# A windowed nearest-neighbour attention block: keys as weights, and half of a masked add moved from VectorE to ScalarE and GpSimd

## Chip, cores, metric

One core of a Trainium2 chip runs the whole kernel. The metric is device time of one launch in microseconds. Engines are called PE (TensorE), DVE (VectorE), ACT (ScalarE), POOL (GpSimd) and SP (SyncE).

## What is computed

The block works on x of shape 8 x 1024 x 128. Layer norm and modulation come first, then the attention that matters here, for each of 8 heads of width 16; a routed mixture of linear experts follows. The part around the change, cut to its core:

```python
q_h = relu(h @ enc_q[h]); v_h = relu(h @ enc_v[h])
k_windows = q_h[:, idx, :]              # the 64 tokens up to and with t
diff = k_windows - q_h[:, :, None, :]
dist = sqrt((diff * diff * m_h).sum(-1) + 1e-8)
neg_d, loc = top_k(-dist, 32)           # the 32 nearest of 64
infl = exp(-topd); infl = infl / (infl.sum(-1) + 1e-8)
context = einsum('btk,btkd->btd', infl, neighbor_v)
context = context + gate * 0.1 * heb_ctx
out = q_h * context                     # then @ decoder, residual, norm, experts
```

## The kernel before

After a prologue (norm, projections, routing) the tokens are worked in 64 chunks of 128. All engines run a software pipeline written out by hand: step i of an engine's `step` function holds work of chunks i-3 to i+3, in a fixed order, and semaphores are all that ties the engines. A buffer has two copies (index s) or four (s4). An engine takes its instructions strictly in order, so an instruction that waits holds up all behind it.

The way of one chunk k, with the lines of the profile:

- PE writes squared distances of 128 queries to 192 keys, for 8 heads, into psD (`distances`, L1142 and L1145). A mask is added by a first matmul. For each query, the 64 keys of its window lie in an outer block (64 columns; left for the first 64 queries, right for the rest) and in the middle block. Of each column pair exactly one belongs to the window. The mask adds 1e30 to the one that doesn't, and -1e30 to the token itself.
- ACT copies the outer blocks through Relu into `key` (L666, L667), and the q part into `qh` (L686).
- DVE takes the minimum of `key` and the middle block, all eight heads in one instruction of 512 columns out of PSUM (L1012). This stands in the middle of step k-1, after two of the four rounds of picking.
- ACT forms `key` = (distance squared) to the power 1/4 with a Ln and an Exp (L701, L727).
- DVE, step k: four rounds of MAX8 (L979, 8 heads) and MATCH_REPLACE (L990, 8 heads) take out the 32 largest keys, which are the 32 farthest, and put -1e4 in their place in `work`. Semaphore `picked` tells when four heads are through.
- ACT, step k+1: Square and Exp(-x) of `work`, four heads at a time (L628, L635, `square` and `weights`), give exp(-distance) for the near ones and 0 for those taken out.
- POOL, step k+1: `unfold` (L452) spreads four heads' weights over 128 key columns.
- PE transposes these weights (L1161), ACT copies them out (L642, `to_wts`), PE multiplies them with the values (L1175).
- ACT copies the context (`cst`, L714, L715) and forms 1/sum with a Ln and an Exp (`den` L717, `rden` L733).
- POOL, step k+1: context times q (`t1`, L481), and the Hebbian part in two products (`t2`, L483, L485); step k+2: `t1` times `rden` (L461), plus `t2` (L465), to `osp`, which goes to the decoder on PE.

In step i POOL's order is L461, L465 (chunk i-2), two unfolds (i-1), `sqs` L475 (i+3), L481, L483, L485 (i-1), `selm` L491 (i+3), `hsc` L497 (i), `sst` L502 (i+3), and two small ones, L509 and L510 (i+2). ACT's order in step i begins with square and weights of chunk i-1, then `h2T` (L658), the outer copies of chunk i+1, `yo` (L673), and so on. ACT's waits for the right to overwrite `key` and for `yo` read:

```python
act.wait_ge(dist_ready, k + 1)
need(act, picked, 16 * (k - 2) + 4)
```

The second is reached when the first of the four rounds has read `key` of chunk k-2.

## Time and profile before

| What | us |
|---|---|
| Median of 3 runs | 816.1 |
| Lowest and highest run | 813.3, 819.37 |
| The profiled execution, its time | 814.3 |
| Its span, first to last instruction | 812.5 |
| DVE busy | 759.0 |
| PE busy | 705.3 |
| ACT busy | 678.9 |
| POOL busy | 465.8 |
| DVE in the chain that ended last | 83% of the span |

Start times are from the span's start. A record of DVE, ACT or PE can run a little past the start of the next one, since instructions are pipelined; what an instruction costs a busy engine is the distance from its start to the next start. The row of an instruction that waited says in brackets how long and for whom. The granted TensorE clock was 0.958 of full speed over the span and 1.00 in the steady part.

### The profile page before, as it was taken

The numbers are of one execution on the slowest core, as the hardware profiler recorded it, in microseconds if no ns is written. First come the engines' busy times: TensorE is split into PE (matmuls) and PEld (weight loads), VectorE is DVE, ScalarE is ACT, GpSimd is POOL, SyncE is SP. The second block draws the span as 40 slices with busy tenths as digits, with TensorE's granted clock in tenths as the row PEclk, the third lists the DMA queues.
The fourth block names the chain that finished last, engine by engine and source line by source line (L and its number), as shares of the span: only waits on it lengthen the run. The fifth ranks groups of instructions, "written<-read, shape, count | busy, mean of one in ns | idle before, by whom it ended". The sixth has DMA issues, their size and how long they took to land.

```text
span 812.5 us, 21167 instructions
## 1 busy us (share of the span) xinstructions
PE 705.3 (87%) x4437; PEld 577.8 (71%) x4437; DVE 759.0 (93%) x6490; ACT 678.9 (84%) x2182; POOL 465.8 (57%) x871
## 2 busy tenths in 40 slices
PE   5987989999898889988988899889888998898844
PEld 3445667777777777777777777777777777777743
DVE  5956899999999999999999999999999999999980
ACT  3981359988888998898989988898999888988964
POOL 2112456666666666666666666666666666666541
PEclk9995989999999999999999999999999999999955
DMA  5310000111111001111110011111100111111000
GB/s 171 107 31 10 25 17 27 32 32 32 33 31 31 27 26 32 32 32 32 31 31 27 26 32 33 33 31 31 31 25 29 32 31 32 32 31 31 19 4 10
DMA packets 49232, 27.23 MB, mean 34 GB/s; under 512 B 5513, under 2 KB 48593, under 8 KB 49105
## 3 DMA queue, kind: packets, MB, share of 16 engines
q1 hardware_dynamic: 49104, 25.90, 10.9%
q14 instruction: 92, 0.75, 0.3%
q8 instruction: 36, 0.59, 0.3%
HBM read 10.28 MB, written 4.19 MB: 18 GB/s over the span
## 4 chain that ended last, share of the span: by engine, by line
DVE 83%; PE 9%; ACT 2%; DMA 2%; issue 1%; POOL 1%; SPq 1%; ACTq 0%; POOLq 0%
DVE work L990 46%; DVE m L979 30%; DVE key L1012 5%; DMA big<-in_x 1%; PE psD L1145 1%; DVE key L801 1%; PE psD L1050 1%; DVE st_p L792 1%; PE psC L1175 1%; PE psC L1078 1%; PE psW L1232 1%; PE psW L1161 1%; DMA wmod_sb<-in_wmod 1%; POOL big L452 1%; PE psX L1133 0%
## 5 line engine op out<-in xcount | busy, mean ns | idle before, releaser
L990 DVE MATCH_REPLACE8 work<-m,work 128x64 f32<-128x64 f32 x1536 | 301.0, 208 | 0.0
L1145 PE MATMUL psD<-sst,tst 128*128 128x224 f32 x1024 | 238.7, 356 | 0.0
L979 DVE MAX8 m<-work 128x8 f32<-128x64 f32 x1536 | 211.5, 210 | 0.0
L1145 PEld LDWEIGHTS psD<-sst,tst 128*128 128x128 f32 x1024 | 196.5, 192 | 3.1 <-issue 0.3
L452 POOL TENSOR_TENSOR big<-work,con 128x512 f32<-128x512 f32 x128 | 162.2, 1290 | 20.5 <-ACT work L635 15.9
L481 POOL TENSOR_TENSOR t<-cst,qh 128x128 f32<-128x128 f32 x64 | 27.7, 433 | 213.2 <-ACT cst L715 213.2
L1175 PE MATMUL psC<-vst,big 128*128 128x34 f32 x1024 | 127.5, 270 | 0.0
L1175 PEld LDWEIGHTS psC<-vst,big 128*128 128x128 f32 x1024 | 126.8, 195 | 0.2
L990 DVE MATCH_VALUE_LOAD work<-m,work 128x8 f32 x1536 | 122.3, 80 | 0.0
L990 DVE MATCH_REPLACE8 work<-m,key 128x64 f32<-128x64 f32 x512 | 100.2, 208 | 0.0
L1142 PE MATMUL psD<-mask_bf,ident_bf 128*128 128x448 bf16 x256 | 91.5, 357 | 1.8 <-DMA tst<-nst 1.8
L1161 PE MATMUL psW<-con,big 128*128 128x128 f32 x512 | 79.9, 280 | 2.9 <-POOL big L452 2.9
L701 ACT ACTIVATE key<-key,bias 128x512 f32<-128x512 f32 x64 | 46.2, 722 | 40.2 <-DVE key L1012 40.2
L642 ACT ACTIVATE big<-psW 128x512 f32<-128x512 f32 x128 | 76.1, 595 | 3.1 <-PE psW L1161 2.9
L1232 PE MATMUL psW<-sqs,selm 128*8 128x192 f32 x256 | 53.3, 332 | 21.9 <-POOL selm L491 21.9
L979 DVE MAX8 m<-key 128x8 f32<-128x64 f32 x512 | 70.5, 209 | 0.0
L1161 PEld LDWEIGHTS psW<-con,big 128*128 128x128 f32 x512 | 58.6, 144 | 4.2 <-POOL big L452 4.1
L502 POOL TENSOR_TENSOR sst<-qT_all,aS 128x384 f32<-128x384 f32 x64 | 53.1, 830 | 12.4 <-PE psD L1145 12.4
L635 ACT ACTIVATE work<-work 128x256 f32<-128x256 f32 x128 | 53.4, 417 | 4.1
L1232 PEld LDWEIGHTS psW<-sqs,selm 128*8 128x8 f32 x256 | 17.9, 89 | 54.2 <-POOL selm L491 41.1
L1183 PE MATMUL psX<-x,con 128*128 128x128 f32 x128 | 32.5, 337 | 27.0 <-ACT h2T L658 27.0
L475 POOL TENSOR_TENSOR sqs<-qT_all 128x384 f32<-128x384 f32 x64 | 54.1, 846 | 1.6 <-ACT qT_all L565 1.5
(200 smaller groups left out, 1473.6 us busy)
## 6 DMA issues: line engine op xcount, KB each, us to landing
hst<-hT_all SPq DMA_DIRECT2D x64, 96.0 KB
tst<-qT_all SPq DMA_DIRECT2D x256, 17.0 KB
big<-in_x SPq DMA_DIRECT2D x16, 256.0 KB, 2.8
tst<-nst SPq DMA_DIRECT2D x256, 1.0 KB
xs<-in_x SPq DMA_DIRECT2D x64, 64.0 KB, 1.9
out<-yo SPq DMA_DIRECT2D x64, 64.0 KB, 1.7
sst<-nst SPq DMA_DIRECT2D x128, 3.0 KB
con<-in_consts SPq DMA_DIRECT2D x1, 549.5 KB, 6.7
```

The source lines that it names most:

```text
L452: nc.gpsimd.tensor_tensor(wun[:, s, heads].rearrange("p h (v j) -> p h v j", v=2), work[:, s].rearrange("p (h j) -> p h j", h=NH)[:, heads ...
L475: nc.gpsimd.tensor_tensor(sqs[:, s], win, win, ALU.mult).then_inc(opnd_ready, 1)
L502: nc.gpsimd.tensor_tensor(sst[:, s, :, 0:3 * WIN], qT_all[:, :, bass.ds(column(k), 3 * WIN)], aS[:, :, bass.ds(k // CPB, 1)].broadcast_to( ...
L635: nc.scalar.activation(wk, wk, ACT.Exp, scale=-1.0).then_inc(wsel_ready, 1)
L642: nc.scalar.activation(wts[:, (i - 1) % 2, 4 * w:4 * w + 4].rearrange("p h t -> p (h t)"), psW[:, w], ACT.Copy).then_inc(wts_ready, 1)
L979: last = v.max(m8[:, h], src[:, h * WIN:(h + 1) * WIN])
L990: last = v.match_replace(work[:, s, cols], m8[:, h], src[:, cols], GONE)
L1142: mm(bank_of(r)[:, :, 0:SW], ident_bf[:], mask_bf[:].unsqueeze(1).broadcast_to([P, NG, SW]), start=True, stop=False, skip_group_check=True)
L1145: last = mm(bank_of(r)[:, g, 0:SW], tst[:, s, r, g], sst[:, s, g], start=False, stop=(g == NG - 1), skip_group_check=True)
L1161: nc.tensor.transpose(psW[:, w, (h % 4) * P:(h % 4 + 1) * P], wun[:, s, h], ident).then_inc(wt_ready, 1)
L1175: last = mm(pC[:, h * 2 * VD:(h + 1) * 2 * VD], wts[:, s, h], vst[:, s4, h].rearrange("p v e -> p (v e)"), start=True, stop=True)
L1232: mm(pN, selm[:, s, g], sqs[:, s, g], start=(g == 0), stop=(g == NG - 1))
```

## The change

The functions named below are those of POOL, ACT, DVE and PE in this order; GONE and C_MASK stand at the top.

The key becomes exp(-distance), formed by Ln, Exp(0.5 x) and Exp(-x), so that the 32 largest keys are the nearest. What is taken out is replaced by 0, and the weights are `key` minus `work`, a subtraction on POOL ahead of each unfold; the Square and Exp behind the picking go. The mask is -1e30 throughout: Relu turns the column outside the window into 0, and the minimum becomes a sum. For heads 0 to 3 ACT copies the middle block through Relu into `work`, and POOL adds it to `key`; for heads 4 to 7 DVE adds it from PSUM. The product with q is taken once, after the sum of context and Hebbian part, and not twice.

```diff
-GONE = -1e4
+GONE = 0.0
+ON_POOL = 4
...
-    c[:, C_MASK:C_MASK + 3 * WIN] = np.concatenate([first, middle, last], 1)
+    c[:, C_MASK:C_MASK + 3 * WIN] = -np.abs(np.concatenate([first, middle, last], 1))
...
                         need(pool, wt_ready, 8 * (k - 2) + 4 * w + 4)
+                        heads = slice(4 * w, 4 * w + 4)
+                        wk = work[:, s, w * 4 * WIN:(w + 1) * 4 * WIN]
+                        pool.wait_ge(picked, 16 * k + 15 + w)
+                        nc.gpsimd.tensor_tensor(wk, key[:, s, w * 4 * WIN:(w + 1) * 4 * WIN], wk, ALU.subtract).then_inc(wsel_ready, 1)
                         pool.wait_ge(wsel_ready, 2 * k + 1 + w)
...
-                k, s = i - 2, (i - 2) % 2
+                k, s, s4 = i - 2, (i - 2) % 2, (i - 2) % 4
                 if there(i, -2):
+                    q = qh[:, s4, :, 0:HD]
                     pool.wait_ge(rden_ready, k + 1)
-                    pool.wait_ge(t1_done, k + 1)
-                    nc.gpsimd.tensor_tensor(t1[:].rearrange(h3, h=NH), t1[:].rearrange(h3, h=NH), rden[:, s].unsqueeze(2).broadcast_to([P, NH, HD]), ALU.mult).then_inc(ctx_done, 1)
+                    pool.wait_ge(t2_done, k + 1)
+                    nc.gpsimd.tensor_tensor(t1[:].rearrange(h3, h=NH), cst[:, s, :, 0:HD], rden[:, s].unsqueeze(2).broadcast_to([P, NH, HD]), ALU.mult).then_inc(t1_done, 1)
+                    pool.wait_ge(t1_done, 2 * k + 1)
+                    nc.gpsimd.tensor_tensor(t1[:], t1[:], t2[:, s], ALU.add).then_inc(t1_done, 1)
                     need(pool, po_ready, k - 1)
-                    pool.wait_ge(t2_done, 2 * (k + 1))
-                    pool.wait_ge(ctx_done, k + 1)
-                    nc.gpsimd.tensor_tensor(osp[:, s], t1[:], t2[:], ALU.add).then_inc(osp_ready, 1)
+                    pool.wait_ge(t1_done, 2 * k + 2)
+                    nc.gpsimd.tensor_tensor(osp[:, s].rearrange(h3, h=NH), t1[:].rearrange(h3, h=NH), q, ALU.mult).then_inc(osp_ready, 1)
                 unfold(0)
                 unfold(1)
+
+                k, s = i + 1, (i + 1) % 2
+                if there(i, 1):
+                    pool.wait_ge(outer_ready, 2 * (k + 1))
+                    pool.wait_ge(mid_ready, k + 1)
+                    nc.gpsimd.tensor_tensor(key[:, s, 0:ON_POOL * WIN], key[:, s, 0:ON_POOL * WIN], work[:, s, 0:ON_POOL * WIN], ALU.add).then_inc(d2_ready, 1)
...
-                    q, hb = qh[:, s4, :, 0:HD], qh[:, s4, :, HD:2 * HD]
-                    pool.wait_ge(cst_ready, 2 * (k + 1))
-                    nc.gpsimd.tensor_tensor(t1[:].rearrange(h3, h=NH), cst[:, s, :, 0:HD], q, ALU.mult).then_inc(t1_done, 1)
+                    hb = qh[:, s4, :, HD:2 * HD]
+                    pool.wait_ge(qhs_ready, k + 1)
                     pool.wait_ge(hsc_done, k + 1)
-                    nc.gpsimd.tensor_tensor(t2[:].rearrange(h3, h=NH), hb, hsc[:, s].unsqueeze(2).broadcast_to([P, NH, HD]), ALU.mult).then_inc(t2_done, 1)
-                    pool.wait_ge(t2_done, 2 * k + 1)
-                    nc.gpsimd.tensor_tensor(t2[:].rearrange(h3, h=NH), t2[:].rearrange(h3, h=NH), q, ALU.mult).then_inc(t2_done, 1)
+                    nc.gpsimd.tensor_tensor(t2[:, s].rearrange(h3, h=NH), hb, hsc[:, s].unsqueeze(2).broadcast_to([P, NH, HD]), ALU.mult).then_inc(t2_done, 1)
...
-                square(0)
-                weights(0)
-                square(1)
-                weights(1)
...
-                    need(act, picked, 16 * (k - 2) + 4)
+                    need(act, wsel_ready, 2 * (k - 1))
                     e = key[:, s].rearrange("p (h j) -> p h j", h=NH)
                     nc.scalar.activation(e[0:WIN], pH[0:WIN, :, 0:WIN], ACT.Relu).then_inc(outer_ready, 1)
                     nc.scalar.activation(e[WIN:P], pH[WIN:P, :, 2 * WIN:3 * WIN], ACT.Relu).then_inc(outer_ready, 1)
+                    need(act, w_ready, 2 * (k - 1))
+                    nc.scalar.activation(work[:, s, 0:ON_POOL * WIN].rearrange("p (h j) -> p h j", j=WIN), pH[:, 0:ON_POOL, WIN:2 * WIN],
+                                         ACT.Relu).then_inc(mid_ready, 1)
...
                     act.wait_ge(d2_ready, k + 1)
+                    act.wait_ge(d2b_ready, k + 1)
                     nc.scalar.activation(key[:, s], key[:, s], ACT.Ln, bias=bias[:, 1:2]).then_inc(ln_done, 1)
...
+                    act.wait_ge(ln_done, k + 1)
+                    nc.scalar.activation(key[:, s], key[:, s], ACT.Exp, scale=0.5).then_inc(dist_done, 1)
...
+                    act.wait_ge(dist_done, k + 1)
+                    nc.scalar.activation(key[:, s], key[:, s], ACT.Exp, scale=-1.0).then_inc(key_ready, 1)
...
-                    nc.scalar.activation(key[:, s], key[:, s], ACT.Exp, scale=0.25).then_inc(key_ready, 1)
...
-                    need(act, ctx_done, k - 1)
+                    need(act, osp_ready, k - 1)
                     nc.scalar.activation(rden[:, s], den[:, s], ACT.Exp, scale=-1.0).then_inc(rden_ready, 1)
...
+                    dve.wait_ge(mid_ready, k + 1)
                     dve.wait_ge(qhs_ready, k + 1)
-                    e = key[:, s].rearrange("p (h j) -> p h j", h=NH)
-                    v.scalar_tensor_tensor(out=e, in0=pH[:, :, WIN:2 * WIN], scalar=0.0, in1=e, op0=ALU.max, op1=ALU.min).then_inc(d2_ready, 1)
+                    e = key[:, s].rearrange("p (h j) -> p h j", h=NH)[:, ON_POOL:NH]
+                    v.scalar_tensor_tensor(out=e, in0=pH[:, ON_POOL:NH, WIN:2 * WIN], scalar=0.0, in1=e, op0=ALU.max, op1=ALU.add).then_inc(d2b_ready, 1)
...
-                    need(pe, d2_ready, k)
+                    need(pe, mid_ready, k)
+                    need(pe, qhs_ready, k)
+                    need(pe, d2b_ready, k)
```

On POOL, the beginning of a steady step before the change (`t` stands for t1 or t2, `big` for the unfolded weights `wun`), each with the semaphores it waits for:

```order
L461 TENSOR_TENSOR t<-t,rden 128x128 [waits t1_done,rden_ready]
L465 TENSOR_TENSOR osp<-t 128x128 [waits ctx_done,t2_done,po_ready]
L452 TENSOR_TENSOR big<-work,con 128x512 [waits wsel_ready,wt_ready] x2
L475 TENSOR_TENSOR sqs<-qT_all 128x384 [waits pn_ready]
L481 TENSOR_TENSOR t<-cst,qh 128x128 [waits cst_ready]
L483 TENSOR_TENSOR t<-qh,hsc 128x128 [waits hsc_done]
L485 TENSOR_TENSOR t<-t,qh 128x128 [waits t2_done]
```

The same place after the change:

```order
L467 TENSOR_TENSOR t<-cst,rden 128x128 [waits t2_done,rden_ready]
L469 TENSOR_TENSOR t<-t 128x128 [waits t1_done]
L472 TENSOR_TENSOR osp<-t,qh 128x128 [waits t1_done,po_ready]
L455 TENSOR_TENSOR work<-key,work 128x256 [waits picked,wt_ready]
L457 TENSOR_TENSOR big<-work,con 128x512 [waits wsel_ready]
L455 TENSOR_TENSOR work<-key,work 128x256 [waits picked,wt_ready]
L457 TENSOR_TENSOR big<-work,con 128x512 [waits wsel_ready]
L482 TENSOR_TENSOR key<-key,work 128x256 [waits mid_ready,outer_ready]
L488 TENSOR_TENSOR sqs<-qT_all 128x384 [waits pn_ready]
L495 TENSOR_TENSOR t<-qh,hsc 128x128 [waits hsc_done,qhs_ready]
```

A product moved from the middle to the front, a subtraction stands ahead of each unfold, an addition that waits for ACT stands behind them, and nothing waits for `cst` any more.

On ACT, the copies of the distances in a steady step before, from the picking's results to `qh`:

```order
L628 ACTIVATE work<-work 128x256 [waits picked]
L635 ACTIVATE work<-work 128x256 [waits square_done]
L628 ACTIVATE work<-work 128x256 [waits picked]
L635 ACTIVATE work<-work 128x256 [waits square_done]
L658 ACTIVATE h2T<-psX,modT 128x128 [waits y_ready,pn2_ready]
L666 ACTIVATE key<-psD 64x512 [waits picked,dist_ready]
L667 ACTIVATE key<-psD 64x512
L673 ACTIVATE yo<-psX 128x128 [waits out_in0,y_ready]
```

And after:

```order
L646 ACTIVATE h2T<-psX,modT 128x128 [waits y_ready,pn2_ready]
L654 ACTIVATE key<-psD 64x512 [waits wsel_ready,dist_ready]
L655 ACTIVATE key<-psD 64x512
L657 ACTIVATE work<-psD 128x256 [waits w_ready]
L664 ACTIVATE yo<-psX 128x128 [waits out_in0,y_ready]
L638 ACTIVATE big<-psW 128x512 [waits c_ready,wt_ready]
L671 ACTIVATE oT<-psX 128x128 [waits po_ready]
L677 ACTIVATE qh<-psD 128x256 [waits osp_ready,dist_ready]
```

Four instructions went, one came, and the outer copies and the new middle copy wait for POOL's subtractions and unfolds.

Further on in the same step of ACT, from the key's Ln to `rden`, after the change:

```order
L693 ACTIVATE key<-key,bias 128x512 [waits d2b_ready,d2_ready]
L698 ACTIVATE x,sum_c<-psX,bias 128x128 [waits att_ready]
L704 ACTIVATE key<-key 128x512 [waits ln_done]
L711 ACTIVATE cst<-psC 64x136 [waits osp_ready,c_ready]
L712 ACTIVATE cst<-psC 64x136
L714 ACTIVATE den<-cst,bias 128x8 [waits cst_ready]
L719 ACTIVATE key<-key 128x512 [waits dist_done]
L724 ACTIVATE nm_c<-sum_c 128x1 [waits x2_ready]
L730 ACTIVATE rden<-den 128x8 [waits osp_ready,den_done]
```

Before, the same stretch held one Exp of `key` instead of two, between `nm_c` and `rden`.

## Rows read from the trace of the kernel before

**Rows 1.** The page: busy time, share of the span and instructions of each engine.

```profile
PE 705.3 (87%) x4437; PEld 577.8 (71%) x4437; DVE 759.0 (93%) x6490; ACT 678.9 (84%) x2182; POOL 465.8 (57%) x871
```

**Rows 2.** Busy time of each engine in stretches, the first the ramp, the others ten steps.

```profile
core 0: us, PE busy (x) PEld busy (x) DVE busy (x) ACT busy (x) POOL busy (x), PEclk, DMA share, GB/s
109.00:205.00 96.00, 87.45 (x566) 73.88 (x567) 94.55 (x848) 83.49 (x270) 61.58 (x116) 0.97 0.09 28
205.00:313.50 108.50, 97.68 (x661) 83.10 (x660) 108.50 (x971) 98.09 (x320) 70.24 (x131) 1.00 0.10 30
...
639.00:747.50 108.50, 97.65 (x662) 83.15 (x662) 108.50 (x971) 98.06 (x321) 70.24 (x131) 1.00 0.10 31
```

**Rows 3.** Waits of POOL: engine, line, waited for: us in total, times, longest.

```profile
POOL t L481 <- ACT cst L715: 213.2, 64, 6.6
```

**Rows 4.** Timeline of DVE, one step: start us, us, engine line op out<-in.

```profile
408.84 1.11 DVE L979 MAX8 m<-key 128x8 f32<-128x64 f32 x8
...
413.97 0.69 DVE L1012 SCALAR_TENSOR_TENSOR key<-psD,key 128x512 f32<-128x512 f32 x1
414.57 1.11 DVE L979 MAX8 m<-work 128x8 f32<-128x64 f32 x8
...
418.79 0.22 DVE L990 MATCH_REPLACE8 work<-m,work 128x64 f32<-128x64 f32 x1
...
419.70 1.11 DVE L979 MAX8 m<-key 128x8 f32<-128x64 f32 x8
```

**Rows 5.** Timeline of POOL in the same step; in brackets the idle time before.

```profile
409.75 2.54 POOL L452 TENSOR_TENSOR big<-work,con 128x512 f32<-128x512 f32 x2
412.24 0.83 POOL L475 TENSOR_TENSOR sqs<-qT_all 128x384 f32<-128x384 f32 x1
416.31 0.43 POOL L481 TENSOR_TENSOR t<-cst,qh 128x128 f32<-128x128 f32 x1 [3.24 <-ACT cst L715]
416.70 0.40 POOL L483 TENSOR_TENSOR t<-qh,hsc 128x128 f32<-128x128 f32 x1
417.18 0.45 POOL L485 TENSOR_TENSOR t<-t,qh 128x128 f32<-128x128 f32 x1
...
419.49 0.40 POOL L461 TENSOR_TENSOR t<-t,rden 128x128 f32<-128x128 f32 x1
420.06 0.46 POOL L465 TENSOR_TENSOR osp<-t 128x128 f32<-128x128 f32 x1 [0.17 <-POOL t L461]
420.60 2.52 POOL L452 TENSOR_TENSOR big<-work,con 128x512 f32<-128x512 f32 x2
```

**Rows 6.** Timeline of ACT in the same step.

```profile
410.61 0.58 ACT L666 ACTIVATE key<-psD 64x512 f32<-64x512 f32 x1
...
411.83 0.28 ACT L673 ACTIVATE yo<-psX 128x128 f32<-128x128 f32 x1
...
412.76 0.38 ACT L686 ACTIVATE qh<-psD 128x256 f32<-128x256 f32 x1
413.04 0.60 ACT L642 ACTIVATE big<-psW 128x512 f32<-128x512 f32 x1
...
413.83 0.21 ACT L696 ACTIVATE rnn<-lnn 128x8 f32<-128x8 f32 x1
414.69 0.72 ACT L701 ACTIVATE key<-key,bias 128x512 f32<-128x512 f32 x1 [0.66 <-DVE key L1012]
...
415.95 0.28 ACT L715 ACTIVATE cst<-psC 64x136 f32<-64x136 f32 x1
...
416.57 0.61 ACT L727 ACTIVATE key<-key 128x512 f32<-128x512 f32 x1
417.09 0.19 ACT L733 ACTIVATE rden<-den 128x8 f32<-128x8 f32 x1
```

**Rows 7.** Timeline of PE in the same step.

```profile
414.99 0.35 PE L1142 MATMUL psD<-mask_bf,ident_bf 128*128 128x448 bf16 x1
...
420.31 0.92 PE L1145 MATMUL psD<-sst,tst 128*128 128x224 f32 x4
```

More of the change, by code:

```diff
@@ L172, in adaln_block @@
         t1 = sb("t1", [P, NH * HD])
-        t2 = sb("t2", [P, NH * HD])
+        t2 = sb("t2", [P, 2, NH * HD])
         osp = sb("osp", [P, 2, NH * HD])
@@ L269, in adaln_block @@
         outer_ready = sem("outer_ready")
+        mid_ready = sem("mid_ready")
         d2_ready = sem("d2_ready")
+        d2b_ready = sem("d2b_ready")
         ln_done = sem("ln_done")
@@ L275, in adaln_block @@
         picked = sem("picked")
-        square_done = sem("square_done")
+        dist_done = sem("dist_done")
         wsel_ready = sem("wsel_ready")
@@ L294, in adaln_block @@
         t2_done = sem("t2_done")
-        ctx_done = sem("ctx_done")
         osp_ready = sem("osp_ready")
@@ L449, in unfold @@
                         need(pool, wt_ready, 8 * (k - 2) + 4 * w + 4)
+                        heads = slice(4 * w, 4 * w + 4)
+                        wk = work[:, s, w * 4 * WIN:(w + 1) * 4 * WIN]
+                        pool.wait_ge(picked, 16 * k + 15 + w)
+                        nc.gpsimd.tensor_tensor(wk, key[:, s, w * 4 * WIN:(w + 1) * 4 * WIN], wk, ALU.subtract).then_inc(wsel_ready, 1)
                         pool.wait_ge(wsel_ready, 2 * k + 1 + w)
-                        heads = slice(4 * w, 4 * w + 4)
                         nc.gpsimd.tensor_tensor(
@@ L622, in step @@
             def step(i):
-                def square(w):
-                    if there(i, -1):
-                        wk = work[:, (i - 1) % 2, w * 4 * WIN:(w + 1) * 4 * WIN]
-                        act.wait_ge(picked, 16 * (i - 1) + 15 + w)
-                        nc.scalar.activation(wk, wk, ACT.Square).then_inc(square_done, 1)
-                def weights(w):
-                    if there(i, -1):
-                        wk = work[:, (i - 1) % 2, w * 4 * WIN:(w + 1) * 4 * WIN]
-                        act.wait_ge(square_done, 2 * (i - 1) + 1 + w)
-                        nc.scalar.activation(wk, wk, ACT.Exp, scale=-1.0).then_inc(wsel_ready, 1)
                 def to_wts(w):
@@ L707, in step @@
                                          accum_out=sum_c[:, s:s + 1]).then_inc(x2_ready, 1)
+                k, s = i + 1, (i + 1) % 2
+                if there(i, 1):
+                    act.wait_ge(ln_done, k + 1)
+                    nc.scalar.activation(key[:, s], key[:, s], ACT.Exp, scale=0.5).then_inc(dist_done, 1)
                 k, s = i - 1, (i - 1) % 2
@@ L717, in step @@
                     nc.scalar.activation(den[:, s], cst[:, s, :, HD], ACT.Ln, bias=bias[:, 1:2]).then_inc(den_done, 1)
+                k, s = i + 1, (i + 1) % 2
+                if there(i, 1):
+                    act.wait_ge(dist_done, k + 1)
+                    nc.scalar.activation(key[:, s], key[:, s], ACT.Exp, scale=-1.0).then_inc(key_ready, 1)
                 k, s = i - 2, (i - 2) % 2
@@ L722, in step @@
                     nc.scalar.activation(nm_c[:], sum_c[:, s:s + 1], ACT.Copy, scale=-1.0 / D).then_inc(nm_done, 1)
-                k, s = i + 1, (i + 1) % 2
-                if there(i, 1):
-                    act.wait_ge(ln_done, k + 1)
-                    nc.scalar.activation(key[:, s], key[:, s], ACT.Exp, scale=0.25).then_inc(key_ready, 1)
                 k, s = i - 1, (i - 1) % 2
```

## Prediction

> **What bounds the kernel now.** I read the page's busy times first. DVE leads with 93% of the span, ahead of PE with 87% [rows 1]; a share over the span can't say who holds up whom. The busy times by stretch can: from 205 us to 747 us DVE is busy for 108.50 of 108.50 us, ten steps at a time, with PE at 97.7, ACT at 98.1, POOL at 70.2 and the granted clock at 1.00 [rows 2]. In the ramp, 109 to 205 us, DVE had 1.45 us idle [rows 2]. One step lasts 419.70 - 408.84 = 10.86 us on DVE's timeline [rows 4]; ten steps give 10.85, and I use that. So DVE alone sets the pace. Everything else has slack, POOL most: it waits 213 us in total for `cst`, 3.24 us of each step [rows 3, 5].
>
> **DVE by itself.** The instruction that shrinks from 512 to 256 columns starts at 413.97, and the next starts at 414.57, so it costs 0.60 us [rows 4]. Its duration less the fixed part goes by columns. I take 0.34 us for half (bounds: 0.30, the plain half, and 0.60, unchanged). The 64 searches and replacements of a step are untouched; what is replaced, and by what, changes no shape. DVE's own step becomes 10.85 - 0.26 = 10.59 us. If nothing else moved, the kernel would gain 64 x 0.26 = 17 us.
>
> **What now closes in a ring.** Before, ACT could copy the outer blocks of chunk i+1 as soon as the distances were there. Its wait for `picked` was for the first round of chunk i-1, long past. After, `key` and `work` of chunk i-1 are read by POOL after the picking, so in step i the outer copies wait for both subtractions, and the middle copy waits for both unfolds. Behind this middle copy in ACT's queue stand `yo`, both weight copies, `qh`, the Ln, both Exps, `cst`, `den` and `rden`. POOL's first instruction of step i+1 waits for `rden` of step i, and the next subtraction stands three instructions behind it. So POOL's step i releases ACT's step i, which releases POOL's step i+1: a ring with no DVE in it. Its length is a lower bound for the step, so I add it up. S is the start of the first subtraction.
>
> POOL, from S to the end of the second unfold. The subtraction on 128x256 is not in this trace. Its bounds are 0.40 us, the product on 128x128, and 0.83, the one on 128x384 [rows 5]. Half of an unfold of 512 columns (2.54/2 = 1.27 each) is 0.64, about midway, and I take it. A POOL instruction that waits for the one before it starts late: the product at 416.70 lasts 0.40, and its follower starts at 417.18, 0.08 late [rows 5]. The unfolds start 2.49/2 = 1.25 us apart [rows 5]. Sum: 0.64 + 0.08 + 1.25 + 0.64 + 0.08 + 1.27 = 3.96.
>
> The Trainium skill bears on this term ("GPSIMD Engine Reference", section 3.1): a two-input tensor_tensor on GPSIMD takes about 2.6 cycles of 1.2 GHz per element, and section 4.1 advises VectorE for elementwise adds, about twice as fast. Estimated from that page, 256 columns take 0.55 us before any fixed part; with 0.55 in both places the ring below would be 0.18 shorter, and the kernel 11 us faster than my sum. The rows agree with its direction: POOL pays 0.64 for the add for which DVE saves 0.26.
>
> Hand-over to ACT: I take 0.08, that of ACT to POOL, whose `cst` record ends at 415.95 + 0.28 = 416.23 while POOL starts at 416.31 [rows 5, 6]. The outer copies don't count: they start after the second subtraction, last 411.83 - 410.61 = 1.22 [rows 6], and the unfold beside them takes 1.35 with its hand-over. The ring goes through the unfold.
>
> ACT, from the middle copy to the end of `rden`. The middle copy is 128x256 out of PSUM, like `qh`, whose follower starts 413.04 - 412.76 = 0.28 later [rows 6]; the other end is half of the two outer copies, 0.61. I take 0.28 for the equal shape. From `yo` at 411.83 to the end of `rnn` at 413.83 + 0.21 it is 2.21 [rows 6]; today ACT then idles 0.66 for DVE [rows 6], which here falls into the ring. From the Ln at 414.69 to `rden` at 417.09 it is 2.40; `rden` lasts 0.19; the second Exp costs what the first does, 417.09 - 416.57 = 0.52 [rows 6]. Sum: 0.28 + 2.21 + 2.40 + 0.52 + 0.19 = 5.60. Then 0.08 back to POOL.
>
> POOL, from `rden` to the next subtraction: 0.40 + 0.08 for the first product, 0.46 for the add, with a gap of 0.17 as ahead of today's `osp`, and 420.60 - 420.06 = 0.54 for the third [rows 5]. Sum 1.65.
>
> Ring: 3.96 + 0.08 + 5.60 + 0.08 + 1.65 = 11.37 us, against 10.85 today and 10.59 for DVE alone.
>
> **Does anything on the ring wait still longer?** DVE's half: `qh` ends 412.76 + 0.38 - 411.83 = 1.31 after `yo` starts, so at S + 3.96 + 0.08 + 0.28 + 1.31 = S + 5.63, and DVE can add at S + 5.68. With 0.34 it is done at S + 6.02, before ACT comes to the Ln at S + 6.53. POOL's add, ready 0.64 + 0.08 after the middle copy, is earlier. From the add to the next step DVE needs 419.70 - 414.57 = 5.13 [rows 4], so the next step starts at S + 11.15. The first half of the picks is out 419.70 - 418.79 - 0.22 = 0.69 before the end, at S + 10.46, and POOL wants it at S + 11.37. DVE is off the ring by 0.9 us, and has 11.37 - 10.59 = 0.78 us idle per step, at its add, waiting for `qh`. PE: from the first distances at 414.99 to the end of the last at 420.31 + 0.92 it is 6.24 [rows 7]. The first distances keep their place 414.99 - 411.83 = 3.16 behind `yo`, since all ahead of them hangs on `yo` and the weight copies as before. So the distances end 9.40 behind `yo`, and the outer copies want them 11.37 - 0.28 - 1.35 = 9.74 behind it. That is 0.34 of slack, and the wait of PE for `selm` inside the stretch goes, since `selm` no longer stands behind `cst`. POOL itself: 1.65 and 3.96 on the ring, then 0.08 + 0.38 + 0.08 for the middle copy, 0.64 for the add, 0.83 for `sqs`, 0.48 for `t2`, and 419.49 - 417.18 - 0.41 = 1.90 for `selm` to `n2g` [rows 5] make 10.0, which is 1.4 short of the ring; its wait for `cst` (3.24) is gone. ACT has its remaining 2.8 us (norm, `vst`, `nst`, `h2T`) beside POOL's part and idles there.
>
> **Sum.** The ring holds from step 2, the first with a `rden` to wait for, to step 62, the last with a next chunk: 61 steps x (11.37 - 10.85) = +31.7 us. Steps 0 and 1 run at DVE's new pace: -0.5. DVE's lead over POOL, 0.9, is used up once: -0.9. The 1.45 us that DVE idled in the ramp [rows 2] falls together with the new waits: -1.5. The prologue and the tail I put at nothing: one more Exp and a POOL add ahead of chunk 0 (+1.2) against Squares and Exps that go in the tail (about -1). Total +28.8. The profiled execution took 814.3, so it would take 843.1. The median of the runs lay 1.8 above it: 845 us.
>
> **Ends of the unknown costs.** Subtractions at 0.40 or 0.83: -0.48 or +0.38 per step. Middle copy at 0.61: +0.33. The four gaps and hand-overs of 0.08 at nothing or at 0.17: -0.32 or +0.36. All low gives 10.57, all high 12.44. They won't err together: I hold 11.1 to 11.7 likely, which is 829 to 865 us.
>
> **Rivals.** (A) DVE stays the bound. For it speaks that DVE is the only full engine today, and that its load shrinks by 0.26; against it, that the ring would have to be 0.78 shorter than its rows. Below a ring of 10.59 the time is 816.1 - 16.6 = 799.5, faster than before. It takes almost all low ends together: chance 0.07. (B) The ring comes out near today's step, 10.7 to 11.0, because gaps that I counted overlap: then losses and savings cancel within 1%, which is about what a measurement of this kernel can tell from no change. About 817 us, chance 0.09. (C) The ring is longer, by subtractions at 0.83 and a middle copy at 0.61: 11.37 + 0.38 + 0.33 = 12.08, 61 x 1.23 - 2.9 = +72, 888 us. Against it is the shape of `qh`. With cases in between, chance 0.07. (D) PE idles longer in one piece per step (after the first transposes, until `yo`, over 1 us against 0.34 now), and the granted clock falls from 1.00. Then PE, 97.7 of 108.5 us busy at full clock [rows 2], would itself set a step beyond 12 us: over 890 us, chance 0.02.
>
> **How the numbers follow.** The forecast has 0.75. Slower by over 1% is the forecast, C and D: 0.84; within 1% is B: 0.09; faster is A: 0.07. The range goes from 818, about the middle of B, to 866, the top of the likely ring; 0.07 + 0.04 lies below and 0.09 above.
>
> **What would show it.** Right: DVE busy about 93% in the steady stretches, its idle time at the new add (L1010), put down to ACT's `qh` copy; ACT idle ahead of the outer or middle copy, waiting for POOL; POOL idle ahead of L467, waiting for `rden`, instead of `cst`; a step of 11.2 to 11.6 us. Wrong: DVE still without idle time between 205 and 740 us; POOL waiting for `picked`; a POOL subtraction far from 0.64; or a second wait inside the ring, ahead of the Ln or of `cst`.

## The result, and the profile after

The changed kernel takes 879.38 us (median of 4 runs, 877.85 to 882.29) against 814.95 us for the kernel before (813.3 to 819.37). The ratio is 1.081, with a 95% interval of 1.077 to 1.084: slower, as forecast, but by 64 us where 29 were forecast, and outside the range of 818 to 866 us. The profiled execution spans 878.3 us; its granted TensorE clock is 0.892 where it was 0.958. All ratios below are to the kernel before, run beside each variant; its medians lay between 812.2 and 815.8 us.

The page of the changed kernel: busy times, the chain, and the groups with idle time ahead of them (busy, mean ns of one | idle before, and for whom).

```profile
PE 743.5 (85%) x4437; PEld 630.4 (72%) x4437; DVE 744.7 (85%) x6490; ACT 651.5 (74%) x2054; POOL 575.3 (66%) x999
...
PE 34%; POOL 27%; ACT 26%; issue 8%; DVE 3%; DMA 2%; ACTq 0%; POOLq 0%; SPq 0%; DVEq 0%
...
L467 POOL TENSOR_TENSOR t<-cst,rden 128x128 f32<-128x128 f32 x64 | 25.7, 401 | 116.0 <-ACT rden L730 116.0
L482 POOL TENSOR_TENSOR key<-key,work 128x256 f32<-128x256 f32 x64 | 46.9, 733 | 81.4 <-ACT work L657 81.4
...
L1190 PE MATMUL psX<-con,osp 128*128 128x128 f32 x64 | 19.6, 307 | 94.7 <-ACT yo L664 94.7
L455 POOL TENSOR_TENSOR work<-key,work 128x256 f32<-128x256 f32 x128 | 93.3, 729 | 2.3 <-PE psX L1131 2.3
L1010 DVE SCALAR_TENSOR_TENSOR key<-psD,key 128x256 f32<-128x256 f32 x64 | 27.2, 425 | 78.4 <-ACT qh L677 78.4
```

DVE, 93% busy in [rows 1], is down to 85%, and the chain that ended last runs over PE, POOL and ACT instead. The waits stand where the ring has its joints: POOL waits for `rden` (116.0 us, in place of the 213 us for `cst` of [rows 3]), and its add for the middle copy; DVE waits 78.4 us at its add for `qh`. One wait I had passed over quickly is large too: PE idles 94.7 us ahead of the transpose of `osp` (L1190, called the osp transpose below), until ACT has copied `yo`. And L455, the subtraction, lasts 729 ns.

Busy times of the changed kernel by stretch, columns as in [rows 2]: one of 108.5 us, then two steps that follow each other, from `yo` to `yo`.

```profile
core 0: us, PE busy (x) PEld busy (x) DVE busy (x) ACT busy (x) POOL busy (x), PEclk, DMA share, GB/s
205.00:313.50 108.50, 94.51 (x597) 83.24 (x596) 95.97 (x872) 84.78 (x272) 78.91 (x136) 0.91 0.09 27
```

```profile
403.53:414.74 11.21, 9.43 (x66) 8.40 (x66) 9.80 (x89) 9.31 (x31) 8.73 (x15) 1.00 0.10 30
414.74:428.56 13.82, 12.73 (x66) 11.40 (x66) 11.57 (x106) 9.65 (x32) 8.76 (x15) 0.75 0.08 23
```

and a piece of the second of them:

```profile
416.90:422.50 5.60, 5.60 (x23) 5.36 (x24) 5.60 (x53) 3.72 (x14) 2.46 (x8) 0.50 0.10 30
```

In [rows 2] the steady stretches had a granted clock of 1.00. Here it is 0.91. The two single steps show why: the first lasts 11.21 us at 1.00, the next 13.82 at 0.75, with a piece of 5.60 us at 0.50. I call a step at 1.00 throughout a full-clock step, and the stretch at 0.50 a fall of the clock. So the steps are of several kinds. From the starts of `yo` (L664) in ACT's timeline I took the length of all steps up to the last few: 59 steps, of which 39 last 11.20 to 11.24 us, one 11.40, 15 last 13.8, and 4 last 12.2. Nearly all steps of the kernel before last 10.84 to 10.87 us. The account: 59 x (11.22 - 10.85) = 21.8 us for the longer step, and 15 x 2.58 + 4 x 0.95 = 42.5 us for steps with a fall of the clock, together 64.3 us. The medians differ by 64.4 us, the spans of the two profiled executions by 65.8; ramp and tail make up the small rest.

The full-clock step, and the slow one behind it, on ACT:

```profile
403.53 0.27 ACT L664 ACTIVATE yo<-psX 128x128 f32<-128x128 f32 x1
...
405.64 0.71 ACT L693 ACTIVATE key<-key,bias 128x512 f32<-128x512 f32 x1
...
408.54 0.19 ACT L730 ACTIVATE rden<-den 128x8 f32<-128x8 f32 x1
...
413.18 0.59 ACT L654 ACTIVATE key<-psD 64x512 f32<-64x512 f32 x1 [1.13 <-POOL work L455]
...
414.46 0.38 ACT L657 ACTIVATE work<-psD 128x256 f32<-128x256 f32 x1
414.74 0.27 ACT L664 ACTIVATE yo<-psX 128x128 f32<-128x128 f32 x1
...
427.05 0.59 ACT L654 ACTIVATE key<-psD 64x512 f32<-64x512 f32 x1 [0.48 <-PE psD L1143]
...
428.56 0.27 ACT L664 ACTIVATE yo<-psX 128x128 f32<-128x128 f32 x1
```

and the same ring on POOL:

```profile
408.81 0.40 POOL L467 TENSOR_TENSOR t<-cst,rden 128x128 f32<-128x128 f32 x1 [1.38 <-ACT rden L730]
...
410.30 0.73 POOL L455 TENSOR_TENSOR work<-key,work 128x256 f32<-128x256 f32 x1
411.11 1.28 POOL L457 TENSOR_TENSOR big<-work,con 128x512 f32<-128x512 f32 x1
412.35 0.73 POOL L455 TENSOR_TENSOR work<-key,work 128x256 f32<-128x256 f32 x1
413.16 1.27 POOL L457 TENSOR_TENSOR big<-work,con 128x512 f32<-128x512 f32 x1
```

These rows give the ring term by term. From the first subtraction (410.30) to the middle copy (414.46) it is 4.16 us, where I had 3.96 + 0.08. From there to `yo` 0.28, as taken. From `yo` (403.53) to the Ln (405.64) 2.11 for 2.21, and from the Ln to the end of `rden` (408.73) 3.09 for 3.11. Then 0.08 to POOL, and from L467 (408.81) to the subtraction (410.30) 1.49 for 1.65. Sum 11.21 for 11.37.

In the slow step the joint is another one. ACT's outer copy at 427.05 waits 0.48 us for PE, not for POOL as at 413.18. PE shows what happened:

```profile
411.58 0.92 PE L1143 MATMUL psD<-sst,tst 128*128 128x224 f32 x4
...
415.16 0.30 PE L1190 MATMUL psX<-con,osp 128*128 128x128 f32 x1 [1.78 <-ACT yo L664]
...
419.82 1.70 PE L1143 MATMUL psD<-sst,tst 128*128 128x224 f32 x4
```

The four distance matmuls of one bank took 0.92 us at 411.58; at 419.82, after the idle time of 1.78 us, they took 1.70. In the full-clock step PE's last distances end 411.58 + 0.92 - 403.53 = 8.97 behind `yo`, and ACT's outer copies start 413.18 - 403.53 = 9.65 behind it, so 0.68 us is to spare. In the slow step ACT can start only 427.05 - 414.74 = 12.31 behind `yo`, because PE isn't done. With 1.51 for the outer and middle copies that makes 13.82.

The idle time before the osp transpose is not the same in all steps. In PE's timeline it is 1.8 us, as the 1.78 above, in nearly all of the 40 steps that follow a full-clock one, and 1.1 us in the 19 that follow a slow one; the mean of 1.55 (94.7 / 61) mixes the two. Of the 40, 19 are slow; of the 19, none.

### The profile page after: what moved, and what is told of

Same layout as the page of the kernel before. It is cut to its first block, busy times and chain, and to the rows that moved or that the text cites. A ratio compares the mean times of both kernels' runs of the same rounds, so it can differ in the third digit from the quotient of the medians.

```text
span 878.3 us, 21484 instructions
## 1 busy us (share of the span) xinstructions
PE 743.5 (85%) x4437; PEld 630.4 (72%) x4437; DVE 744.7 (85%) x6490; ACT 651.5 (74%) x2054; POOL 575.3 (66%) x999
## 4 chain that ended last, share of the span: by engine, by line
PE 34%; POOL 27%; ACT 26%; issue 8%; DVE 3%; DMA 2%; ACTq 0%; POOLq 0%; SPq 0%; DVEq 0%
POOL big L457 13%; PE psD L1143 10%; POOL work L455 7%; PE psC L1173 6%; ACT big L638 5%; ACT key L693 3%; ACT key L719 3%; PE psD L1140 3%; ACT key L704 2%; PE psW L1232 2%; POOL t L469 2%; POOL osp L472 2%; PE psW L1219 2%; POOL t L467 2%; ACT qh L677 2%
## 5 line engine op out<-in xcount | busy, mean ns | idle before, releaser
L1143 PE MATMUL psD<-sst,tst 128*128 128x224 f32 x1024 | 262.2, 383 | 0.0
L1143 PEld LDWEIGHTS psD<-sst,tst 128*128 128x128 f32 x1024 | 214.6, 210 | 7.2 <-issue 0.3
L1173 PE MATMUL psC<-vst,big 128*128 128x34 f32 x1024 | 144.5, 291 | 2.7 <-ACT big L638 2.7
L1173 PEld LDWEIGHTS psC<-vst,big 128*128 128x128 f32 x1024 | 144.4, 218 | 3.1 <-issue 3.1
L467 POOL TENSOR_TENSOR t<-cst,rden 128x128 f32<-128x128 f32 x64 | 25.7, 401 | 116.0 <-ACT rden L730 116.0
L482 POOL TENSOR_TENSOR key<-key,work 128x256 f32<-128x256 f32 x64 | 46.9, 733 | 81.4 <-ACT work L657 81.4
L1190 PE MATMUL psX<-con,osp 128*128 128x128 f32 x64 | 19.6, 307 | 94.7 <-ACT yo L664 94.7
L455 POOL TENSOR_TENSOR work<-key,work 128x256 f32<-128x256 f32 x128 | 93.3, 729 | 2.3 <-PE psX L1131 2.3
L1010 DVE SCALAR_TENSOR_TENSOR key<-psD,key 128x256 f32<-128x256 f32 x64 | 27.2, 425 | 78.4 <-ACT qh L677 78.4
L1190 PEld LDWEIGHTS psX<-con,osp 128*128 128x128 f32 x64 | 9.1, 143 | 107.5 <-issue 107.5
L654 ACT ACTIVATE key<-psD 64x512 f32<-64x512 f32 x64 | 37.8, 591 | 62.0 <-POOL work L455 46.6
```

What stands on the lines that cost most here:

```text
L455: nc.gpsimd.tensor_tensor(wk, key[:, s, w * 4 * WIN:(w + 1) * 4 * WIN], wk, ALU.subtract).then_inc(wsel_ready, 1)
L467: nc.gpsimd.tensor_tensor(t1[:].rearrange(h3, h=NH), cst[:, s, :, 0:HD], rden[:, s].unsqueeze(2).broadcast_to([P, NH, HD]), ALU.mult).then ...
L482: nc.gpsimd.tensor_tensor(key[:, s, 0:ON_POOL * WIN], key[:, s, 0:ON_POOL * WIN], work[:, s, 0:ON_POOL * WIN], ALU.add).then_inc(d2_ready, 1)
L1143: last = mm(bank_of(r)[:, g, 0:SW], tst[:, s, r, g], sst[:, s, g], start=False, stop=(g == NG - 1), skip_group_check=True)
L1173: last = mm(pC[:, h * 2 * VD:(h + 1) * 2 * VD], wts[:, s, h], vst[:, s4, h].rearrange("p v e -> p (v e)"), start=True, stop=True)
```

## Experiments

**The gap filled (e1).** The first question was whether PE's idle time brings the clock down. Against the changed kernel, on PE behind `weights_T(0)`:

```diff
+                if there(i, -3) and there(i, -1):
+                    need(pe, cst_ready, 2 * (i - 1))
+                    for _ in range(12):
+                        nc.tensor.transpose(psC[:, 0:P], ident, ident)
```

> The changed kernel, and PE runs 12 idle transposes of the identity into psC (their output is never read) after the first weight transposes, where it waits for ACT's copy yo. Theory (ring of POOL and ACT of 11.22 us per step, and on top of it a fall of the granted clock brought on by PE's idle stretch ahead of the osp transpose): the 15 steps of 13.80 us and the 5 of 12.17 us become 11.22 us, so 15 x 2.58 + 5 x 0.95 = 43 us less than 879, about 836 us, clock near 0.96. Rival 1 (the clock falls for another reason, such as the lower load of PE over the step): 870 us or more. Rival 2 (the transposes cost what they last, 1.3 us per step, since PE is on the path): 879 + 80 = 960 us.

Measured: 838.03 us, ratio 1.032 (1.027 to 1.037). All steady steps lie between 11.21 and 11.40 us. Ten steps' worth of time, and what is left of the wait:

```profile
422.00:530.50 108.50, 103.39 (x758) 93.74 (x757) 102.62 (x933) 90.10 (x288) 84.24 (x145) 1.00 0.10 30
```

```profile
PE psX L1195 <- ACT yo L664: 30.6, 61, 0.7
```

The clock is at 1.00 and 41 us of the 64 are gone, although PE does 1.3 us more per step. Rival 2 falls. Rival 1 is not excluded by this run alone, since the transposes fill the gap and raise PE's load over the step at once (103.39 of 108.50 us busy, for 94.51); e2 and the last two runs bear on it. The ring's part, the step of 11.24, is untouched.

**The ring opened (e2).** The second question was whether the two waits for overwriting are what closes the ring. The buffer for the middle block lies in a tile of the prologue (`wmod_sb`), since SBUF was full, and so does now `sq_c`, a small work buffer of the norm. Chunk k has its key in `key[:, k % 3]`; against the changed kernel:

```diff
-        key = sb("key", [P, 2, NH * WIN])
+        key = sb("key", [P, 3, NH * WIN])
...
+        midb = wmod_sb[:, 0:2 * ON_POOL * WIN].rearrange("p (s c) -> p s c", s=2)
...
-                    need(act, wsel_ready, 2 * (k - 1))
+                    need(act, wsel_ready, 2 * (k - 2))
...
-                    need(act, w_ready, 2 * (k - 1))
+                    need(act, d2_ready, k - 1)
-                    nc.scalar.activation(work[:, s, 0:ON_POOL * WIN].rearrange("p (h j) -> p h j", j=WIN), pH[:, 0:ON_POOL, WIN:2 * WIN],
+                    nc.scalar.activation(midb[:, s].rearrange("p (h j) -> p h j", j=WIN), pH[:, 0:ON_POOL, WIN:2 * WIN],
```

> The changed kernel with three copies of key and a buffer of its own for the middle block, so that ACT's copies in step i wait for nothing that POOL does in step i. Instructions and their order are those of the changed kernel. Theory (the two overwrite waits close the ring): DVE is full again at 10.59 us per step, PE's idle stretch goes and the granted clock stays at 1.00; 64 x 0.26 = 17 us below before, 798 to 804 us. Rival (the later weights, by way of subtraction, unfold, transposes, contexts and rden, or POOL's load of 10 us a step, set the pace by themselves): a step of 11 us or more, 825 us or more.

Measured: 807.38 us, ratio 0.993 (0.990 to 0.996). The same instructions in the same order, 72 us faster than with two copies of `key`. But it is 3 us over the expected range, and the clock was not at 1.00 throughout:

```profile
422.00:530.50 108.50, 96.94 (x662) 85.78 (x663) 108.05 (x991) 95.74 (x303) 88.28 (x152) 0.98 0.11 31
```

```profile
346.93 0.27 ACT L665 ACTIVATE yo<-psX 128x128 f32<-128x128 f32 x1
...
359.14 0.27 ACT L665 ACTIVATE yo<-psX 128x128 f32<-128x128 f32 x1
```

DVE is nearly full. Most steps last 10.5 to 10.6 us; five of 58 last 12.2, as that from 346.93 to 359.14. PE still idled 1.07 us a step ahead of the osp transpose (65.5 us in 61 waits).

This run also says something on rival 1 above. A full-clock step of the kernel before, with its three waits on PE, and then one of e2:

```profile
411.83:422.68 10.85, 9.77 (x67) 8.32 (x66) 10.85 (x99) 9.81 (x33) 7.04 (x14) 1.00 0.10 30
```

```profile
417.86 0.82 PE L1232 MATMUL psW<-sqs,selm 128*8 128x192 f32 x4 [0.36 <-POOL selm L491]
...
421.61 0.49 PE L1183 MATMUL psX<-x,con 128*128 128x128 f32 x2 [0.38 <-ACT h2T L658]
...
423.10 0.30 PE L1192 MATMUL psX<-con,osp 128*128 128x128 f32 x1 [0.34 <-ACT yo L673]
```

```profile
390.68:401.19 10.51, 9.43 (x66) 8.40 (x66) 10.51 (x98) 9.37 (x31) 8.63 (x16) 1.00 0.10 30
```

PE is busy for 90% of the step in both, and idle for 1.08 us in both. Before, this idle time stands in three places and no step is slow; in e2 it stands in one, and five are. So a lower load of PE over the step isn't needed for a fall; what differs is how the idle time is spread. Of the growth from 0.34 to 1.07 us the middle copy ahead of `yo` accounts for about 0.27 (0.61 in e3, below); the rest is what PE no longer waits elsewhere.

**Both at once (e5).** So I filled that gap too, with 8 transposes.

> e2_no_ring and 8 idle transposes of PE ahead of the osp transpose, where it idles 1.07 us a step. Theory: the 7 steps of 12.2 us in e2 were falls of the clock behind that idle stretch and go; all steps 10.5 to 10.6 us, 807 - 7 x 1.6 = 796 us, clock 0.96 or more. Rival (those steps come from something else, or 0.9 us more of PE's work delays the path): 807 us or more.

Measured: 796.67 us, ratio 0.980 (0.976 to 0.983): faster than both kernels. DVE is full and the clock at 1.00:

```profile
422.00:530.50 108.50, 106.38 (x759) 95.28 (x758) 108.50 (x996) 96.47 (x306) 89.75 (x154) 1.00 0.11 31
```

The five long steps are gone; all steady ones last 10.51 to 10.69. PE is at 106.38 of 108.50, so there is little room for more such filling. That the time came out at the expected 796 is in part luck: the expectation counts seven long steps in e2, where the trace has five, 8.6 us longer together. The profiled spans differ by 10.0 us, of which 6.4 lie in the 58 steady steps and 3.5 ahead of them.

**One part alone (e3).** The half add was then put into the kernel before, with a buffer of its own for the middle block. POOL adds behind `unfold(1)`, ACT copies behind the outer copies, and DVE adds heads 4 to 7; against the kernel before:

```diff
-    c[:, C_MASK:C_MASK + 3 * WIN] = np.concatenate([first, middle, last], 1)
+    c[:, C_MASK:C_MASK + 3 * WIN] = -np.abs(np.concatenate([first, middle, last], 1))
...
+                    pool.wait_ge(mid_ready, k + 1)
+                    nc.gpsimd.tensor_tensor(key[:, s, 0:ON_POOL * WIN], key[:, s, 0:ON_POOL * WIN], midb[:, s], ALU.add).then_inc(d2p_ready, 1)
...
+                    need(act, d2p_ready, k - 1)
+                    nc.scalar.activation(midb[:, s].rearrange("p (h j) -> p h j", j=WIN), pH[:, 0:ON_POOL, WIN:2 * WIN],
+                                         ACT.Relu).then_inc(mid_ready, 1)
...
+                    v.scalar_tensor_tensor(out=e, in0=pH[:, ON_POOL:NH, WIN:2 * WIN], scalar=0.0, in1=e, op0=ALU.max, op1=ALU.add).then_inc(d2_ready, 1)
```

> The kernel before with one part of the change alone: the mask negative throughout, the middle block of heads 0 to 3 copied by ACT (into a buffer of its own) and added on POOL, heads 4 to 7 added on DVE. Key, Square and Exp stay as before. Theory (half an add on DVE is worth 0.26 us a step as long as no wait takes its place): step of 10.59 us, 798 to 804 us, DVE without idle time. Rival (ACT, with 0.66 us idle before and 0.28 more to do, or the wait of the Ln for POOL's add, takes it back): 812 us or more.

Measured: 804.79 us, ratio 0.990 (0.986 to 0.994); a step of 10.67 us. The saving is real, but the step is 0.08 us longer than expected, and the time 0.8 us above the expected range:

```profile
429.08 1.11 DVE L993 MAX8 m<-work 128x8 f32<-128x64 f32 x8
...
431.72 0.42 DVE L1026 SCALAR_TENSOR_TENSOR key<-psD,key 128x256 f32<-128x256 f32 x1
```

```profile
431.31 0.38 ACT L699 ACTIVATE qh<-psD 128x256 f32<-128x256 f32 x1
```

Two rounds of DVE take 419.70 - 414.57 = 5.13 us [rows 4], one 2.56, so DVE could have added at 429.08 + 2.56 = 431.64; it starts at 431.72, when the record of `qh` has ended at 431.69. `qh` comes 0.28 later than before, behind the middle copy. The price of the copy shows on DVE, and not on ACT.

**The other part alone (e4).** The exp(-distance) key with its subtractions on POOL, and the whole add on DVE, whose waits for `mid_ready` go with ACT's for `d2_ready`; against the changed kernel:

```diff
-                    need(act, w_ready, 2 * (k - 1))
-                    nc.scalar.activation(work[:, s, 0:ON_POOL * WIN].rearrange("p (h j) -> p h j", j=WIN), pH[:, 0:ON_POOL, WIN:2 * WIN],
-                                         ACT.Relu).then_inc(mid_ready, 1)
...
-                    nc.gpsimd.tensor_tensor(key[:, s, 0:ON_POOL * WIN], key[:, s, 0:ON_POOL * WIN], work[:, s, 0:ON_POOL * WIN], ALU.add).then_inc(d2_ready, 1)
...
-                    v.scalar_tensor_tensor(out=e, in0=pH[:, ON_POOL:NH, WIN:2 * WIN], scalar=0.0, in1=e, op0=ALU.max, op1=ALU.add).then_inc(d2b_ready, 1)
+                    v.scalar_tensor_tensor(out=e, in0=pH[:, :, WIN:2 * WIN], scalar=0.0, in1=e, op0=ALU.max, op1=ALU.add).then_inc(d2b_ready, 1)
```

> The changed kernel with the whole middle block added on DVE out of PSUM, no middle copy and no add on POOL; the key as exp(-distance) and the subtractions on POOL stay. Theory: the ring goes on through the second subtraction and the outer copies, and is shorter by 1.28 + 0.28 - 1.22 = 0.34 us, 10.88 us, level with DVE's 10.85: 816 to 825 us if the clock holds, up to 850 where it falls in some steps, with PE still idle over 1 us ahead of the osp transpose. Rival (the middle copy and its wait for the unfolds are the whole loss): DVE full, no fall of the clock, 815 us and PE idle ahead of that transpose as before, 0.34 us.

Measured: 850.66 us, ratio 1.046 (1.041 to 1.050). The full-clock step is 10.88 us, as worked out, so at full clock this kernel would be level with the one before. But 11 steps last 13.5 us and 3 last 11.9. PE idles 78.3 us in 61 waits: 1.45 us in a step behind a full-clock one, 0.81 behind a slow one. So more than half of the loss (4.6 of 8.1%) is there without the split add. It comes with the rest of the change, which holds the new key with its wait for the subtractions, but also POOL's moved product; this run doesn't part the two.

**The fall without the change (e6, e7).** If PE's gap is the cause, it must work in the kernel before as well, with nothing of the change in it. In ACT's order `to_wts(0)` and `qh` move ahead of `yo` and `oT`:

```diff
+                to_wts(0)
...
+                    nc.scalar.activation(qh[:, s4], pQH, ACT.Copy).then_inc(qhs_ready, 1)
...
                     nc.scalar.activation(yo[:, s], pY, ACT.Copy).then_inc(yo_ready, 1)
-                to_wts(0)
...
                     nc.scalar.activation(oT[:, s], pO, ACT.Copy).then_inc(oT_ready, 1)
...
-                    nc.scalar.activation(qh[:, s4], pQH, ACT.Copy).then_inc(qhs_ready, 1)
```

> The kernel before with one reordering on ACT: yo and oT come after the first weight copy and qh, 0.87 us later. Nothing of the change is in it. PE's idle stretch ahead of the osp transpose grows from 0.34 to about 1.2 us. Theory: the granted clock falls in some steps although DVE, ACT and POOL do the same work as before. At full clock the way from yo through PE's distances (9.04 to 9.40) back to the outer copies and to yo (1.22 + 0.87) is 11.1 to 11.5 us, and steps with a fall come on top, 10 to 45 us over e7_before_late_yo_filled. Rival (the fall in the changed kernel has to do with its other work): no fall here, the same time as e7.

> e6_before_late_yo and 8 idle transposes of PE in its idle stretch. Theory: no fall of the clock, every step at its full-clock length of 11.1 to 11.5 us, 828 to 852 us, and 10 to 45 us less than e6. Rival: as e6, or slower.

Measured: 867.48 us for e6 (ratio 1.067, 1.063 to 1.071) and 840.85 for e7 (1.034, 1.031 to 1.038), a difference of 26.6 us. PE in e6, three steps that follow each other, each with the osp transpose and then the distances of the second bank:

```profile
284.06 0.30 PE L1192 MATMUL psX<-con,osp 128*128 128x128 f32 x1 [1.22 <-ACT yo L681]
...
288.38 0.92 PE L1145 MATMUL psD<-sst,tst 128*128 128x224 f32 x4
...
295.34 0.30 PE L1192 MATMUL psX<-con,osp 128*128 128x128 f32 x1 [1.22 <-ACT yo L681]
...
301.70 1.70 PE L1145 MATMUL psD<-sst,tst 128*128 128x224 f32 x4
...
309.86 0.30 PE L1192 MATMUL psX<-con,osp 128*128 128x128 f32 x1 [1.22 <-ACT yo L681]
...
314.18 0.92 PE L1145 MATMUL psD<-sst,tst 128*128 128x224 f32 x4
```

The gap is 1.22 us in each step, and the distances take 0.92, 1.70, 0.92 us. Six of the 58 steady steps last 14.5 to 14.7 us, every tenth one, and the rest 11.28. In e7, where the gap is filled, all last 11.27 to 11.37:

```profile
422.00:530.50 108.50, 101.77 (x720) 89.14 (x721) 105.19 (x933) 95.12 (x308) 66.68 (x123) 1.00 0.10 30
```

6 x 3.25 = 19.5 of the 26.6 us are these steps; the rest lies in the ramp and the tail, where e6 is longer too. The full-clock step of 11.28 lies in the expected range, but not for the reason given there. ACT in one such step of e6:

```profile
389.17 0.28 ACT L686 ACTIVATE oT<-psX 128x128 f32<-128x128 f32 x1 [0.48 <-PE psX L1192]
...
397.59 0.58 ACT L666 ACTIVATE key<-psD 64x512 f32<-64x512 f32 x1
```

The outer copies (397.59) don't wait for PE's distances. ACT idles 0.48 us ahead of `oT`, 0.18 ahead of the second weight copy and 0.20 ahead of `cst`, each time for PE, which starts late behind the later `yo`; otherwise its queue is full. So the price of the later `yo`, 10.85 to 11.28, is paid on ACT.

**Is it a ring (e8, e9)?** One more addition of 128x256 on POOL, its output unused: in e8 on the ring, ahead of `unfold(0)`, with 18 transposes in the gap; in e9 beside it, ahead of `hsc`, with 12. Against e1_filled_gap both have:

```diff
+                if there(i, -1):
+                    nc.gpsimd.tensor_tensor(wmod_sb[:, 512:768], wmod_sb[:, 0:256], wmod_sb[:, 256:512], ALU.add)
```

> e1_filled_gap with one more addition of 128x256 on POOL (its output is not used) ahead of the first subtraction, that is on the ring, and 18 idle transposes instead of 12. Theory: every step is longer by what the addition lasts, 0.69 to 0.73 us: 11.24 + 0.71 = 11.95 us, 838 + 61 x 0.71 = 881 us. Rival (POOL isn't on the path): 838 to 845 us.

> e1_filled_gap with the same addition on POOL at another place, ahead of hsc, where POOL afterwards waits about 1.5 us for rden. Theory: the ring doesn't go through it, 11.24 us a step and 838 us as e1; POOL's wait for rden shrinks by 0.7 us. Rival (POOL is limited by its load as a whole): 881 us as e8.

Measured: e8 884.85 us (ratio 1.085), nearly every step 11.92 us, 0.68 more than in e1. e9 837.28 us (ratio 1.027), nearly every step 11.24 as in e1. The waits of POOL for `rden` in e8 and in e9:

```profile
POOL t L467 <- ACT rden L733: 102.3, 64, 6.5
```

```profile
POOL t L467 <- ACT rden L733: 54.9, 63, 4.5
```

In e1 it was 99.4 us. Beside the ring the addition is paid out of this wait (54.9 left); on the ring it is paid in full by every step. POOL's load as such costs nothing here.

**Moving `yo` instead of filling the gap (e10, e11).** In the changed kernel (e10) and in e2 (e11) `yo` was put right behind `h2T`, ahead of the outer copies.

> The changed kernel with yo copied by ACT right behind h2T, ahead of the outer copies, so that the osp transpose no longer waits for the middle copy. Theory (idle time of PE in one piece brings the clock down, wherever it stands): yo leaves the ring (0.16 us), a full-clock step is 11.06 us; PE now idles over 1 us ahead of the second weight transposes, whose unfold ends late, and falls of the clock stay: 835 to 875 us. Rival (it is this place, the osp transpose, that matters): no steps over 12 us, 826 us.

> e2_no_ring with yo moved in the same way and no idle transposes. ACT's copies wait for nothing of POOL here, so the osp and second weight transposes can run while ACT copies the distances, and PE's idle time is split: 0.5 us or less ahead of each. Theory: no falls of the clock, DVE full, 795 to 799 us as e5. Rival (ACT loses by waiting for PE's pY before its outer copies, 0.6 us a step): 810 us or more.

Measured: e10 863.87 us (ratio 1.061, 1.056 to 1.066), within the range of the theory; its full-clock step is 10.92, 0.14 less than expected. e11 868.83 us (1.069, 1.064 to 1.073): a miss, and my rival was right, with more on top. In e11, ACT first, then PE in two steps that follow each other, and a full-clock step:

```profile
413.87 0.28 ACT L654 ACTIVATE yo<-psX 128x128 f32<-128x128 f32 x1 [0.93 <-PE psX L1183]
```

```profile
405.36 1.05 PE L1174 MATMUL psC<-vst,big 128*128 128x34 f32 x8 [1.20 <-ACT big L639]
...
415.30 0.66 PE L1160 MATMUL psW<-con,big 128*128 128x128 f32 x4 [0.70 <-POOL big L458]
416.28 1.05 PE L1174 MATMUL psC<-vst,big 128*128 128x34 f32 x8 [0.33 <-ACT big L639]
...
418.91 1.70 PE L1144 MATMUL psD<-sst,tst 128*128 128x224 f32 x4
```

```profile
437.39:448.31 10.92, 9.87 (x68) 8.44 (x67) 10.68 (x99) 9.20 (x31) 8.74 (x16) 1.00 0.10 30
```

ACT now waits 0.93 us for PE's pY before it may copy `yo` and then the distances, and a full-clock step is 10.92 us where e2 had 10.5 to 10.6. In e10 ACT waits as long for the same (61.1 us in 64 waits in both), and the step is the same; by what way it closes I did not follow up.

PE's idle time was split, but not as expected: in a step behind a full-clock one it is 0.70 us ahead of the second weight transposes and 0.33 ahead of the contexts, with 0.66 us of work between them. The one piece of 1.20 us at 405.36 stands in a step behind a slow one. Falls came behind the split pair too: the distances at 418.91 took 1.70 us, and the step from 413.87 lasts 12.59. In both e10 and e11, 22 of the 58 steady steps are slow, at 12.6 or 14.2 us, and 39 of these 44 have the split pair. Yet PE is busy for 9.87 of 10.92 us in a full-clock step, 90% as in the kernel before. So the fall doesn't hang on the osp transpose, nor on a lower load of PE. And the theory's "in one piece" is too narrow: two pieces close together did it as well.

## Why the prediction went wrong

- What bounds the kernel before, and DVE's own saving: right. DVE's add costs 0.34 us (404.94 to 405.28 in its timeline), and e5's steps are 10.58 us on average, for 10.59.
- The ring: right in path and length. 11.22 us for 11.37 predicted; e2 opens it, e8 and e9 show what lies on it and what doesn't. With the clock held up (e1) the changed kernel takes 838 us, where the sum said 845.
- Its terms: the subtraction was mis-sized, 0.73 for 0.64, twice. It was made good by POOL's front products (1.49 for 1.65) and by ACT's stretch up to the Ln (2.11 for 2.21).
- DVE's idle time at its add, waiting for `qh`, and POOL's wait for `rden`: right in place, 78.4 and 116.0 us in all.
- The step that failed is rival D, "PE idles longer in one piece per step ... and the granted clock falls from 1.00". I saw the mechanism and its place, gave it 0.02, and put the clock at nothing in the sum. I took it as all or nothing: at the lower level throughout, or never. In fact it falls in 19 of 59 steps and comes back each time; in the one shown it is at 0.50 for all of the 5.60 us from 416.90. The falls cost 42.5 us. That is more than the 34 us by which the time exceeds the sum of 845, since the ring itself came out 0.15 us a step shorter than forecast, about 9 us in all.
- The second fault is in the paragraph on PE. It counted 0.34 us of slack for the distances and left it there. The trace has 0.68, which is little too, and what PE loses beyond it comes through: ACT's outer copies started 12.31 us behind `yo` instead of 9.65, and the step was 2.61 us longer.
- One of my signs of being wrong did show, in slow steps: a second wait inside the ring. In the one shown, ACT waits 0.57 us for PE ahead of `cst`, at 419.70.
- The Trainium skill ("TensorE: Matmul & The Clock Gate", Part 1) says that the gate follows how busy PE has been and knows two levels, 1.2 and 2.4 GHz. The rows agree: 0.50 of full speed between 416.9 and 422.5 us of the changed kernel, 1.00 in the step before. It would have been the page to weigh.
- Of the page that I did weigh ("GPSIMD Engine Reference", section 3.1, of the Trainium skill) the rate holds: from POOL's add on 128x128 (L469, 0.455 us) to the one on 128x256 (L482, 0.733) it is 2.17 ns per column, and the page's 2.6 cycles make the same. What the estimate of 0.55 lacked is the fixed part; an estimate of it is what is left of L482 over that rate, 0.73 - 0.55 = 0.18 us. My own 0.64 leaned on products that read one operand twice or by broadcast. In the changed kernel POOL's product by broadcast takes 0.40 us on 128x128 (L467) and the operations with two full operands 0.45 (L469, L472), in line with these being the cheaper kind. And where my prediction says that the rows agree with the page's direction, its 0.64 was an estimate; measured, POOL pays 0.73 us for the add for which DVE saves 0.26.
